# A decoder of two layers on one core: the order of VectorE's maxima in the up pass, and the place of three value-product copies

## The chip, the cores and the metric

The kernel runs on one core of a Trainium2 chip. The metric is device time in microseconds of one execution; lower is better. The median of three runs of the kernel before is 1388.31 us (1386.64 to 1389.0).

## The reference, cut to what matters

The whole program is a two-layer decoder on x of 8 x 512 x 256: linear attention, cross attention, a quantized feed-forward (FFN), then a metric attention, a second cross attention and a spectral FFN, each with a residual and a layer norm. The change lies in the feed-forward of layer 0:

```
act_qdq(x): scale = max(max|x| / 32767, 1e-12); clip(round(x / scale), ...) * scale   # one scale for the whole tensor
x    = act_qdq(x)
up   = act_qdq(x @ dequant(w_up).T)          # 8 batches of 512 x 768
gate = act_qdq(x @ dequant(w_gate).T)
sig  = round(sigmoid(gate) * 65536) / 65536, clipped
gate = act_qdq(gate * sig)                   # called t in the kernel before its scale is applied
o    = act_qdq(gate * up)
return o @ dequant(w_down).T
```

Every `act_qdq` needs the largest magnitude over all eight batches before one element can be rounded. That cuts the feed-forward into passes: gate, up, value (the product), down. The second cross attention needs, for each of 16 half head pairs, the product of context values with its output weights ("value products" 0 to 15); these depend on the context alone and are slipped into the passes of the feed-forward.

## The kernel before, in words

Each engine runs a queue of its own in the order in which its function issues work; the order is written out by hand, and engines meet at semaphores.

The **up pass** is the stage of the change. TensorE runs `up_pass(u, middle, after)` for u = 0 to 7: six up products of a batch (j = 0 to 5; each is four matmuls of 128x512 in the profile, L1092), with a small job after the third (middle) or after the sixth (after). Four PSUM banks take the up products in turn, so an up product waits for the copy of the one four before it. The small jobs are the projection of context values, `values(p)` (L1098), and `value_products(n)` (eight matmuls at L1118, two for each value pair), which write banks 6 and 7 and therefore wait until the copy of product n-1 has emptied them.

ScalarE copies the up products out (L1593: "early" is j = 0 to 2, "late" is j = 3 to 5), and between early and late of batch n it rounds the gate of batch n+1 (`gate_round`, L1598) and takes its sigmoid (`ffn_sigmoid`, L1603). Behind the late copies stand `copy_vw(n)` (L1633), which copies value product n to one buffer, and `copy_values(p)` (L1626). `copy_vw` also waits until the store of the product before it has left that buffer. A batch's first up copy waits for the up maximum two batches back, whose buffer it takes, and for its store; `gate_round(n)` waits for t of batch n-2.

VectorE does, for each batch: `gate_product` (L2249, L2250), which needs the batch's sigmoid and makes t in place; `t_peak` (L2255, L2256), the running maximum of t; `up_peak` (L2261, L2264), the running maximum of up, which needs all six up copies of the batch. The last batch's up maximum is taken in halves (`last_up_peak`, L2271). `peak(name)` (L2171) hands a maximum to GpSimd, which shares it over the partitions, and `scale` (L2179 to L2183) makes the scale from it.

SyncE's queue for this stage is: load the x of batch u+2, store up of batch u, store value product 8 + (u - 2), in turn (L621, L626, L561), each issue waiting for its input in this order.

Behind the up pass comes the **value stage**: ScalarE rounds up and t (L1701, L1693), VectorE multiplies them and takes the maximum (L2301, L2304), the last value products and the keys of the second cross attention are made beside it, and everything in it starts from the up scale. Then the down projection and layer 1 run in one loop over the batches. The value products 13 to 15 stand on ScalarE between the roundings.

Of the kernel before, what the change touches and what calls it, by code (L numbers as in the profile page):

```python
# [24 lines left out]
B, T, C = 8, 512, 256  # L25
# [146 lines left out]
def decoder(nc, x_in, pack_ident, pack_lin, pack_ctx, pack_xat, pack_ffn, pack_l1, pack_prep,  # L172
# [4 lines left out]
    with ctx:  # L177
# [46 lines left out]
        w.update(w1)  # L224
        layer1_end = ar.at
        l1_at = {n: sum(int(np.prod(d)) for _, d in PACK_L1[:i]) for i, (n, _) in enumerate(PACK_L1)}
        met_m = ar.take(NC, P)
        met_wo = ar.take(NC, C)
# [166 lines left out]
        def ev(name):  # L395

            if name not in sems:
                sems[name] = sem(name)
            return sems[name]
# [4 lines left out]
        def sig(name, per=1):  # L404

            if name not in sigs:
                if name in CONTINUES:
                    before = sig(CONTINUES[name], per)
                    sigs[name] = Signal(before.sem, per, before.base + B * per)
                else:  # L410
                    sigs[name] = Signal(sem(name), per)
            assert sigs[name].per == per, name
            return sigs[name]

        def wait(eng, name, b, j=None, per=1):

            s = sig(name, per)
            eng.wait_ge(s.sem, s.at(b, per if j is None else j))
# [28 lines left out]
        def vw_at(n):  # L447

            return 1 + n % 3 if n < VW_AHEAD else 0

        def vw_line(n):

            return ev(f"vw_stored_{max(1, vw_at(n))}")

        def vw_before(n):

            return sum(vw_line(m) is vw_line(n) for m in range(n))
# [5 lines left out]
        def wait_back(eng, name, b, back, per=1):  # L463

            if not b.before(back):
                eng.wait_ge(sig(name, per).sem, sig(name, per).at(b, per * (1 - back)))
# [30 lines left out]
        class Line:  # L497
# [5 lines left out]
            def link(self, ins):  # L503
                self.n += 1
                ins.then_inc(self.sem, 1)
                self.eng.wait_ge(self.sem, self.n)

        def rows2(k, n=2):

            return bank(k, n).rearrange("p a (b c) -> p (a b) c", c=C)  # L510
# [218 lines left out]
        def _(pe):  # L729
# [353 lines left out]
            def ffn_up_product(u, j):  # L1083
                n = NF * u + j
                if j == 0:
                    wait_moved(pe, "xt_loaded", Batch(u), u % 2, 2)
                if n < 4:
                    wait(pe, "gate_copied", Batch(B - 1), n + 1, NF)
                else:
                    wait(pe, "up_copied", Batch(0), n - 3, NF)  # L1090
                for k in range(NC):
                    last = mm(flat(2 + n % 4), wup_t[:, k, j * P:(j + 1) * P], ffn_xt[:, u % 2, k],  # L1092
                              start=k == 0, stop=k == NC - 1)
                last.then_inc(sig("up_done", NF).sem, 1)
# [51 lines left out]
            def up_pass(u, middle=None, after=None):  # L1146

                for j in range(NF):
                    ffn_up_product(u, j)
                    if j == NF // 2 - 1 and middle:  # L1150
                        middle[0](*middle[1:])
                if after:
                    after[0](*after[1:])
# [6 lines left out]
            up_pass(4, after=(values, 5))  # L1160
            up_pass(5, middle=(value_products, 10), after=(value_products, 11))
            up_pass(6, after=(values, 6))
            up_pass(7, middle=(value_products, 12), after=(value_products, 13))


            values(7)
# [279 lines left out]
        def _(act):  # L1446
# [140 lines left out]
            def ffn_copy_up(u, js):  # L1587
                if js[0] == 0:
                    wait_moved(act, "up_stored", Batch(u), u % 2, 2)
                    wait_back(act, "up_peaked", Batch(u), 2)  # L1590
                for j in js:
                    wait(act, "up_done", Batch(u), j + 1, NF)
                    f(ffn_up[:, u % 2, :, j], flat(2 + (NF * u + j) % 4).rearrange("p (t n) -> p t n", t=NT),  # L1593
                      ACT.Copy).then_inc(sig("up_copied", NF).sem, 1)

            def gate_round(n):
                wait_back(act, "t_ready", Batch(n), 2)
                f(gate_i[:, n % 2], gated[:, n], ACT.Copy, scale=quant["gate_mult"])\  # L1598
                    .then_inc(sig("gate_rounded").sem, 1)

            def ffn_sigmoid(n):
                wait(act, "gate_rounded", Batch(n))
                f(gated[:, n], gate_i[:, n % 2], ACT.Sigmoid, scale=quant["gate_scale"])\  # L1603
                    .then_inc(sig("sigmoid_done").sem, 1)
# [23 lines left out]
            def copy_vw(n):  # L1628

                act.wait_ge(ev("vw_done"), n + 1)  # L1630
                if vw_before(n):
                    act.wait_ge(vw_line(n), 32 * vw_before(n))
                f(vw_bufs[vw_at(n)].rearrange("p r i c -> p (r i) c"), rows2(6), ACT.Copy).then_inc(ev("vw_copied"), 1)  # L1633
# [27 lines left out]
            copy_values(4)  # L1661
            ffn_copy_up(3, early)
            gate_round(4)
            ffn_sigmoid(4)
            ffn_copy_up(3, late)
            copy_vw(8)
            ffn_copy_up(4, early)
            gate_round(5)
            ffn_sigmoid(5)
# [2 lines left out]
            copy_values(5)  # L1672
            ffn_copy_up(5, early)
            gate_round(6)
            ffn_sigmoid(6)
            ffn_copy_up(5, late)
            copy_vw(10)
            ffn_copy_up(6, early)
            gate_round(7)
            ffn_sigmoid(7)  # L1680
# [305 lines left out]
        def _(dve):  # L1986
# [183 lines left out]
            def peak(name):  # L2170
                v.tensor_copy(quant[name + "_max"], quant[name + "_max"]).then_inc(ev("peak_found"), 1)  # L2171
# [75 lines left out]
            def gate_product(n):  # L2247
                wait(dve, "sigmoid_done", Batch(n))
                link(v.tensor_scalar(sig_i, gated[:, n], 65536.0, 65535.0, ALU.mult, ALU.min))  # L2249
                v.tensor_tensor(gated[:, n], gate_i[:, n % 2], sig_i, ALU.mult).then_inc(sig("t_ready").sem, 1)  # L2250

            def t_peak(n):
                wait(dve, "t_ready", Batch(n))
                v.memset(spare, 0.0)
                link(v.tensor_reduce(quant["tmp"], gated[:, n], AX.X, ALU.max, apply_absolute_value=True))  # L2255
                link(v.tensor_tensor(quant["t_max"], quant["t_max"], quant["tmp"], ALU.max))  # L2256

            def up_peak(u):
                wait(dve, "up_copied", Batch(u), NF, NF)
                v.memset(spare, 0.0)  # L2260
                v.tensor_reduce(peaks[:, 0:1], ffn_up[:, u % 2].rearrange("p a b c -> p (a b c)"), AX.X, ALU.max,  # L2261
                                apply_absolute_value=True).then_inc(sig("up_peaked").sem, 1)
                wait(dve, "up_peaked", Batch(u))
                link(v.tensor_tensor(quant["up_max"], quant["up_max"], peaks[:, 0:1], ALU.max))  # L2264

            def last_up_peak():
                for n in range(2):
                    wait(dve, "up_copied", Batch(B - 1), NF * (n + 1) // 2, NF)
                    half = ffn_up[:, (B - 1) % 2].rearrange("p t j n -> p t (j n)")[:, :, n * FF // 2:(n + 1) * FF // 2]
                    v.memset(spare, 0.0)  # L2270
                    link(v.tensor_reduce(quant["tmp"], half, AX.XY, ALU.max, apply_absolute_value=True))  # L2271
                    last = v.tensor_tensor(quant["up_max"], quant["up_max"], quant["tmp"], ALU.max)
                    if n == 0:
                        link(last)
                last.then_inc(sig("up_peaked").sem, 1)
                wait(dve, "up_peaked", Batch(B - 1))

            first_gate_product()
            t_peak(0)
            up_peak(0)  # L2280
            for n in range(1, B - 1):
                gate_product(n)
                t_peak(n)
                up_peak(n)
            gate_product(B - 1)
            t_peak(B - 1)
            peak("t")
            last_up_peak()
            peak("up")
            scale("t", quant["t_raw"])  # L2290
# [383 lines left out]
```

## Time and profile before

| | |
|---|---|
| median of the runs | 1388.31 us |
| the profiled execution | 1386.88 us |
| its span, first to last instruction | 1385.1 us |
| mean granted TensorE clock | 0.957 |
| TensorE matmul busy | 1243.0 us (90%) |
| VectorE busy | 1046.8 us (76%) |
| ScalarE busy | 517.6 us (37%) |
| GpSimd busy | 267.7 us (19%) |

The span is the time from the first to the last instruction of one profiled execution, and all times of rows below are microseconds from its start. TensorE's busy share is that of matmuls, whose ends are modelled. The up pass lies between about 475 and 591 us, the value stage runs to about 663 us.

### The profile page before, as it was taken

What the parts mean: (1) busy time and instruction counts of PE and PEld (TensorE: products, weight loads), DVE (VectorE), ACT (ScalarE), POOL (GpSimd) and SP (SyncE); (2) the same over time, 40 slices, a digit from 0 to 9 for tenths busy, and PEclk for the clock granted to TensorE, in tenths of its full rate; (3) what the DMA queues carried; (4) which work ended last, traced back from release to release, by engine and by line L of the source; (5) the groups of instructions that cost most, each with busy time, mean ns of one, the idle gap of its engine ahead of it and who ended that gap; (6) DMA issues with size and microseconds to landing.
All of it is one profiled execution on the core that took longest, in us unless ns stands there. A gap on an engine that the chain in (4) does not pass through costs nothing.

```text
span 1385.1 us, 18416 instructions
## 1 busy us (share of the span) xinstructions
PE 1243.0 (90%) x7325; PEld 831.2 (60%) x7325; DVE 1046.8 (76%) x1949; ACT 517.6 (37%) x608; POOL 267.7 (19%) x189
## 2 busy tenths in 40 slices
PE   7899999997899999853679999999999999998976
PEld 4566666665544554321456686767767686766654
DVE  3578899987534779989554787978878797887767
ACT  1244343443534567588013332232323323241411
POOL 0011111112000000025100322314142141413242
PEclk9899999999999999976799999999999999999988
DMA  5000101102672044489322111111211000000000
GB/s 217 16 16 32 31 1 31 31 16 92 171 272 76 31 166 161 157 308 392 107 82 81 37 54 50 47 45 36 60 56 53 31 24 20 28 19 36 1 16 16
DMA packets 47829, 107.86 MB, mean 78 GB/s; under 512 B 10752, under 2 KB 31360, under 8 KB 44288
## 3 DMA queue, kind: packets, MB, share of 16 engines
q1 hardware_dynamic: 43584, 104.59, 21.7%
q10 hardware_dynamic: 4160, 2.10, 0.5%
q8 instruction: 59, 0.97, 0.3%
q14 instruction: 26, 0.21, 0.0%
HBM read 62.64 MB, written 44.04 MB: 77 GB/s over the span
## 4 chain that ended last, share of the span: by engine, by line
PE 74%; DVE 16%; ACT 4%; issue 2%; DMA 2%; POOL 0%; SPq 0%; POOLq 0%; ACTq 0%; DVEq 0%
PE ps L1313 8%; PE ps L1373 7%; PE ps L1199 6%; PE ps L1041 6%; PE ps L1092 4%; PE ps L795 4%; PE ps L1346 3%; PE ps L1258 3%; PE ps L943 2%; PE ps L1282 2%; PE ps L868 2%; PE ps L1293 2%; PE ps L1420 2%; PE ps L886 2%; PE ps L775 2%
## 5 line engine op out<-in xcount | busy, mean ns | idle before, releaser
L1373 PE MATMUL ps<-arena 128*128 128x256 f32 x512 | 120.3, 389 | 6.7 <-ACT arena L1836 6.7
L1313 PE MATMUL ps<-arena 128*128 128x512 f32 x256 | 117.6, 598 | 0.0
L1373 PEld LDWEIGHTS ps<-arena 128*128 128x128 f32 x512 | 98.5, 194 | 28.1 <-ACT arena L1836 10.0
L1874 POOL TENSOR_TENSOR arena<-arena 128x4 f32<-128x4 f32 x46 | 47.5, 1037 | 306.4 <-DVE arena L2049 306.4
L2389 DVE TENSOR_TENSOR arena<-ps,arena 128x2048 f32<-128x2048 f32 x32 | 73.3, 2291 | 39.1 <-PE ps L1258 38.9
L1935 POOL TENSOR_TENSOR arena<-arena 128x16 f32<-128x16 f32 x32 | 91.9, 2908 | 32.5 <-DVE arena L2418 32.5
L1199 PE MATMUL ps<-arena 128*128 128x256 f32 x384 | 89.4, 390 | 2.8 <-DVE arena L2342 2.8
L1041 PE MATMUL ps<-arena 128*128 128x512 f32 x192 | 85.5, 603 | 1.2 <-ACT arena L1564 1.2
L1092 PE MATMUL ps<-arena 128*128 128x512 f32 x192 | 84.7, 595 | 0.0
L1199 PEld LDWEIGHTS ps<-arena 128*128 128x128 f32 x384 | 73.9, 196 | 13.9 <-issue 3.9
L1313 PEld LDWEIGHTS ps<-arena 128*128 128x128 f32 x256 | 46.2, 190 | 48.7 <-issue 45.1
L1836 ACT ACTIVATE arena<-ps 128x1024 f32<-128x1024 f32 x32 | 32.8, 1026 | 111.9 <-PE ps L1360 111.9
L1346 PE MATMUL ps<-arena 128*128 128x128 f32 x512 | 65.8, 284 | 5.4 <-DVE arena L2432 5.4
L1815 ACT ACTIVATE arena<-ps 128x512 f32<-128x512 f32 x64 | 38.3, 599 | 85.0 <-PE ps L1313 85.0
L2055 DVE TENSOR_SCALAR arena<-arena 128x256 f32<-128x256 f32 x184 | 64.6, 418 | 4.7 <-POOL arena L1874 4.6
L1346 PEld LDWEIGHTS ps<-arena 128*128 128x128 f32 x512 | 62.7, 198 | 7.8 <-DVE arena L2432 7.1
L1881 POOL TENSOR_TENSOR arena<-arena 128x1024 f32<-128x1024 f32 x8 | 18.8, 2354 | 246.4 <-DVE arena L2109 246.4
L1041 PEld LDWEIGHTS ps<-arena 128*128 128x128 f32 x192 | 36.4, 193 | 44.6 <-issue 43.0
L1092 PEld LDWEIGHTS ps<-arena 128*128 128x128 f32 x192 | 36.1, 190 | 43.9 <-issue 41.6
L795 PE MATMUL ps<-arena 128*128 128x512 f32 x128 | 59.2, 597 | 1.3 <-ACT arena L1462 1.3
L2204 DVE TENSOR_REDUCE arena<-arena 128x1 f32<-128x3072 f32 (+1 forms) x9 | 26.9, 2994 | 35.6 <-issue 35.6
L2043 DVE BATCH_NORM_STATS2 arena<-arena 128x6 f32<-128x256 f32 x138 | 49.7, 416 | 4.5 <-POOL arena L1881 2.6
(281 smaller groups left out, 2628.1 us busy)
## 6 DMA issues: line engine op xcount, KB each, us to landing
v_scratch<-arena SPq DMA_DIRECT2D x7, 1536.0 KB, 13.5
arena<-v_scratch SPq DMA_DIRECT2D x7, 1536.0 KB, 6.8
up_scratch<-arena SPq DMA_DIRECT2D x6, 1536.0 KB, 6.6
arena<-up_scratch SPq DMA_DIRECT2D x6, 1536.0 KB, 10.9
vw_scratch<-arena SPq DMA_DIRECT2D x32, 256.0 KB, 3.9
arena<-x_scratch SPq DMA_DIRECT2D x16, 512.0 KB, 4.2
arena<-vw_scratch SPq DMA_DIRECT2D x8, 1024.0 KB
arena<-x SPq DMA_DIRECT2D x8, 512.0 KB, 5.7
```

Source lines behind the costliest of these rows:

```text
L795: last = mm(flat(t % 2), lin_xt[:, par, k, t * P:(t + 1) * P], w["lin_wkv"][:, k], start=k == 0, stop=k == NC - 1)
L1041: last = mm(flat(2 + j), wgate_t[:, k, j * P:(j + 1) * P], ffn_xt[:, par, k], start=k == 0, stop=k == NC - 1)
L1092: last = mm(flat(2 + n % 4), wup_t[:, k, j * P:(j + 1) * P], ffn_xt[:, u % 2, k], start=k == 0, stop=k == NC - 1)
L1199: last = mm(rows2(0 if b.early() else 5)[:, t], dn_v[:, t, j], wdown_t[:, j], start=j == 0, stop=j == NF - 1)
L1313: last = mm(flat(p % 2), w["cos_wq"][:, k, p * P:(p + 1) * P], xt4[:, k], start=k == 0, stop=k == NC - 1)
L1346: last = mm(flat(0, 2)[:, p * P:(p + 1) * P], cos_q[:, p, t * P:(t + 1) * P], cos_kb[:, par, p], start=True, stop=True)
L1373: last = mm(flat(2)[:, C:2 * C], cos_pt[:, p], cos_vw[:, par, p], start=p == 0, stop=p == NP - 1)
L1874: g.tensor_tensor(var[0], var[1], neghalf[:, 0:NT], ALU.pow)\
L1935: g.tensor_tensor(cos_nn[:, t, 0:H], cos_nn[:, t, 0:H], neghalf[:, 0:H], ALU.pow)\
L2043: v.bn_stats(st[:, t], r[:, t])
L2055: last = v.tensor_scalar(y[:, t], r[:, t], mv[:, t, 0:1], rs[:, t:t + 1], ALU.subtract, ALU.mult)
L2389: v.tensor_tensor(met_s[:, n % 2].rearrange("p r t h n -> p (r t h) n"), flat(3, 4).rearrange("p (h n) -> p h n", n=P), w["causal"].unsque ...
```

## The change

On TensorE value product 12 is taken from the middle of the last up pass and put behind it, with product 13 following. On ScalarE the copies of value products 8 and 10 move from behind the late up copies to between the gate's rounding and its sigmoid. On VectorE the up maximum of batch n-1 now follows gate product and t maximum of batch n, for n = 1 to 7; before, the up maximum of batch n followed those of batch n. The t peak is handed over ahead of the up maximum of batch 6. No instruction is added or taken away, and no wait is removed from a function.

```diff
@@ TensorE
             up_pass(6, after=(values, 6))
-            up_pass(7, middle=(value_products, 12), after=(value_products, 13))
+            up_pass(7, after=(value_products, 12))
+            value_products(13)
@@ ScalarE
             gate_round(4)
+            copy_vw(8)
             ffn_sigmoid(4)
             ffn_copy_up(3, late)
-            copy_vw(8)
             ffn_copy_up(4, early)
@@ ScalarE
             gate_round(6)
+            copy_vw(10)
             ffn_sigmoid(6)
             ffn_copy_up(5, late)
-            copy_vw(10)
             ffn_copy_up(6, early)
@@ VectorE
             first_gate_product()
             t_peak(0)
-            up_peak(0)
-            for n in range(1, B - 1):
+            for n in range(1, B):
                 gate_product(n)
                 t_peak(n)
-                up_peak(n)
-            gate_product(B - 1)
-            t_peak(B - 1)
-            peak("t")
+                if n == B - 1:
+                    peak("t")
+                up_peak(n - 1)
             last_up_peak()
             peak("up")
```

## Rows read from the trace of the kernel before

**Rows 1.** Stages: length, busy of PE, PEld, DVE, ACT, POOL; clock, DMA share, GB/s

```profile
487.10:590.60 103.50, 95.98 (x275) 46.59 (x273) 88.86 (x63) 67.15 (x70) 1.25 (x3) 1.00 0.49 167
590.60:662.70 72.10, 29.39 (x81) 15.08 (x81) 66.55 (x53) 55.88 (x30) 27.82 (x9) 0.68 0.89 335
```

**Rows 2.** Waits, 480 to 600 us: total us, times, longest us

```profile
PE ps L1118 <- ACT arena L1633: 13.3, 4, 6.8
DVE arena L2260 <- ACT arena L1593: 13.1, 5, 4.3
```

**Rows 3.** The chain of waits in the up pass: start us, us, what

```profile
531.53 0.92 ACT arena L1633
...
574.27 3.31 DVE arena L2261
```

**Rows 4.** ScalarE in order of time: start us, us, instruction, idle before it

```profile
501.45 2.85 ACT L1603 ACTIVATE arena<-arena 128x3072 f32<-128x3072 int16 x1
...
515.20 2.85 ACT L1603 ACTIVATE arena<-arena 128x3072 f32<-128x3072 int16 x1
...
524.34 2.85 ACT L1598 ACTIVATE arena<-arena 128x3072 int16<-128x3072 f32 x1
527.22 2.86 ACT L1603 ACTIVATE arena<-arena 128x3072 f32<-128x3072 int16 x1
529.98 1.55 ACT L1593 ACTIVATE arena<-ps 128x512 f32<-128x512 f32 x3
531.41 1.03 ACT L1633 ACTIVATE arena<-ps 128x1024 f32<-128x1024 f32 x1
...
542.48 2.85 ACT L1603 ACTIVATE arena<-arena 128x3072 f32<-128x3072 int16 x1
...
548.15 0.62 ACT L1593 ACTIVATE arena<-ps 128x512 f32<-128x512 f32 x1
...
554.50 2.86 ACT L1603 ACTIVATE arena<-arena 128x3072 f32<-128x3072 int16 x1
...
569.76 2.86 ACT L1603 ACTIVATE arena<-arena 128x3072 f32<-128x3072 int16 x1
...
584.82 0.60 ACT L1593 ACTIVATE arena<-ps 128x512 f32<-128x512 f32 x1 [1.12 <-PE ps L1092]
...
592.43 2.85 ACT L1701 ACTIVATE arena<-arena 128x3072 int16<-128x3072 f32 x1 [2.19 <-DVE arena L2183]
```

**Rows 5.** TensorE in order of time, the same columns

```profile
524.80 5.42 PE L1092 MATMUL ps<-arena 128*128 128x512 f32 x12
532.59 1.13 PE L1118 MATMUL ps<-arena 64*128 64x256 f32 x8 [2.37 <-ACT arena L1633]
...
596.34 2.08 PE L1118 MATMUL ps<-arena 64*128 64x256 f32 x8 [6.83 <-ACT arena L1633]
```

**Rows 6.** VectorE in order of time, the same columns

```profile
550.51 1.76 DVE L2249 TENSOR_SCALAR arena<-arena 128x3072 uint16<-128x3072 f32 x1
...
559.29 3.35 DVE L2261 TENSOR_REDUCE arena<-arena 128x1 f32<-128x3072 f32 x1
...
562.87 1.76 DVE L2249 TENSOR_SCALAR arena<-arena 128x3072 uint16<-128x3072 f32 x1
...
586.64 1.75 DVE L2271 TENSOR_REDUCE arena<-arena 128x1 f32<-128x1536 f32 x1
...
590.60 0.15 DVE L2171 COPY arena<-arena 128x1 f32<-128x1 f32 x1
```

**Rows 7.** SyncE's stores of value product 9; landing of these, then of all 32

```profile
547.74 1.18 SPq L561 DMA_DIRECT2D vw_scratch<-arena  x2
...
DMA to landing us min/median/max: 3.3/3.6/3.9
...
DMA to landing us min/median/max: 3.2/3.9/14.2
```

**Rows 8.** TensorE from 596 to 600 us: length, busy, granted clock, DMA share, GB/s

```profile
596.00:600.00 4.00, 3.66 (x10) 0.50 0.91 298
```

## The prediction, made before the changed kernel was run

> **What bounds the kernel now.** I read the busy time by stage first. The stretch from 487.10 to 590.60 us is the one the change edits: 103.5 us, in which TensorE is busy 95.98, VectorE 88.86 and ScalarE 67.15, at full TensorE clock [rows 1]. No engine is full, so the waits come next. Two groups stand out: TensorE's value products waited 13.3 us for the copy of the value product before them (6.83 of it lies after 590 us), and VectorE's up maximum waited 13.1 us, in five pieces, for the last up copies of its batch [rows 2]. The chain of waits shows how they join: it runs over TensorE and ScalarE, passes through the value-product copy at 531.53, and from 574.27 on it is VectorE without a gap [rows 3]. So TensorE and ScalarE set the pace in the middle, and VectorE's backlog sets the end. VectorE idles early for an up maximum whose input isn't there, while the next batch's sigmoid has been ready for some time, and pays this back at the end.
>
> The stage ends where the up peak is found, at 590.60; the scales and the whole value stage hang on it [rows 6].
>
> **Step 1: the copies of value products 8 and 10.** In batch 4's turn ScalarE rounds the gate at 524.34, takes the sigmoid at 527.22, the three late up copies at 529.98 and only then the value-product copy, at 531.41 [rows 4]. TensorE had finished its last up product of that pass at 524.80 + 5.42 = 530.22 and stood 2.37 us for that copy [rows 5]. Value product 8 itself was through by 524.80. After the change the copy starts behind the rounding, at about 527.1, and is done at about 528.1, 2.1 us before TensorE asks. The stall goes. The same pattern repeats one pair later (value product 11, also 2.37), so TensorE is 2.37 us earlier from batch 4's pass on and 4.74 from batch 6's. What is late next on TensorE is the bank rule (an up product needs the copy four products back): its late copies move to about 530.8 to 532.4, and the product that needs the first of them starts at 530.22 + 1.1 + 1.7 = 533.1. It doesn't wait.
>
> The price is paid by the sigmoid. Today it starts 527.22 - 524.34 = 2.88 after the rounding; with the copy between them it starts 2.76 (the pitch from 527.22 to 529.98) + 0.92 (the copy's step in the chain) = 3.68 after. So sigmoids 4 and 6 are 0.8 late against their own rounding. Sigmoid ends, from their starts + 2.85 [rows 4]: 530.08 becomes 530.9; batch 5's 545.33 becomes 542.96; 557.36 becomes 557.36 - 2.37 + 0.8 = 555.8; batch 7's 572.62 becomes 567.9.
>
> **Step 2: VectorE's order.** No instruction is added. The gate product and t maximum of one batch take 559.29 - 550.51 = 8.78 us, the up maximum 562.87 - 559.29 = 3.58, together 12.36 [rows 6]. With the new order the rows give this, a handover from the sigmoid taken at 0.03 (as between the rows at 524.34 and 527.22 of [rows 4]):
> batch 2 starts at sigmoid 501.45 + 2.85 + 0.03 = 504.33 and is through (with up maximum 1) at 516.69; batch 3 waits for its sigmoid, 515.20 + 2.88 = 518.08, until 530.44; batch 4 waits for its sigmoid, starts at 530.9, ends 543.3; batch 5 follows without a wait, to 555.6; batch 6 waits 0.2 for its sigmoid, 555.8, to 568.2; batch 7's product and t maximum end at 576.9, the t peak's copy adds 0.1, up maximum 6 ends at 580.6. The last up maximum in two halves takes 590.60 - 586.64 = 3.96, so the up peak is found at 584.6 instead of 590.6: **6.0 us earlier**.
>
> Each half alone, by the same bookkeeping: only the copies (old VectorE order) gives 586.1, a gain of 4.5, since VectorE still idles for up maximum 3 and again, briefly, for 5; only the order gives 589.0, a gain of 1.6, since sigmoid 7 then still ends at 572.6 and nothing can start before it.
>
> The moved up maximum also frees the up buffer two batches on, and ScalarE waits for that before the batch's first up copy. Up maximum 3 would end at 543.1, and the copy it frees stood at 548.15 [rows 4] and comes at 545.8: 2.7 us to spare, the smallest of these margins. The stores of up to memory read the buffer and wait for nothing of VectorE.
>
> **Step 3: value product 12 behind the last pass.** Its eight matmuls take 1.13 us, as product 9's [rows 5], ahead of the last three up products. Taken out of the middle, the last up copy ends at 585.42 (584.82 + 0.60, [rows 4]) - 4.74 - 1.13 = 579.6. The second half of the last up maximum wants it at 582.6. So this edit is worth nothing to the end, and TensorE and ScalarE have 3 us in hand there. Against it, products 12 and 13 now run one behind the other with a 1.03 us copy between: product 12 to 580.0, copy to 581.0, product 13 to 582.2, the value projection of four matmuls 1.8 more (a third of 5.42, [rows 5]), its copy about 0.7, done at about 584.7. The first rounding of up behind it in ScalarE's queue needs the up scale, 592.43 - 590.60 = 1.8 us after the up peak [rows 4, 6], at 586.4. It is covered by 1.7 us; each microsecond beyond that would come back in full.
>
> **The queues it passes.** SyncE keeps its order. Stores 8 and 10 are issued some 4 to 7 us sooner, and what stands behind them (the load for the next pass) still has TensorE's passes to wait for. ScalarE's new wait is copy 10 for the landing of store 9, one buffer: issued at 547.74 - 2.37 = 545.4, its second half 0.6 later, landing after 3.3 to 3.9 [rows 7], so at 549.9; it is asked for behind the rounding, 554.50 - 0.13 - 2.37 = 552.0 [rows 4]. Margin 2.1 us. Behind that wait stand sigmoid 6 and all of VectorE's last two batches.
>
> **The sum.** The stage ends 6.0 us earlier. Behind it nothing is edited, and all of it starts from the up scale: the value stage (72.1 us, [rows 1]) and the rest of the span should move as one block. Span 1385.1 - 6.0 = 1379.1, the profiled execution's 1386.88 becomes 1380.9, and the median of the runs, 1.4 above that execution, 1388.31 - 6.0 = **1382.3 us**.
>
> The Trainium skill, "Perfetto Trace Analysis", section Identifying the Most-Contended Engine, says to take the engine with the highest occupancy as the bottleneck and close its gaps (for TensorE it warns that matmul busy time flatters). In this stretch that is TensorE with 96 of 103.5 us [rows 1], and its two closed gaps sum to 4.74, where the chain gives 6.0. The rule bears on the first rival.
>
> **Rivals.**
> (a) TensorE's stalls are all there is to win: VectorE's new order brings nothing. Then the time is that of the copies alone, 4.5 us, 1383.8. For it: TensorE is the fullest engine. Against: the chain leaves TensorE at 574.27 [rows 3].
> (b) Only the order works, or the value stage gives back what is won, because the value copy stands in front of the first up rounding (step 3) or because memory traffic binds there (DMA share 0.89, [rows 1]): 1.6 us of gain, 1386.7. Against it: loads and stores of that stage are started by its own roundings and move with them.
> (c) TensorE's clock. Before value product 14 it idled 6.83 us and had fallen to the lower level, 1.2 GHz (0.50), which made that product 2.08 us instead of 1.13 [rows 5, 8], and the key products behind it slower too. I get an idle of about 6.3 us there, so no change. If the clock held, the 3.66 us of matmuls in the four microseconds at 0.50 [rows 8] would take half, 1.8 us more gain, 1380.5; as much again is my bound for what lies behind them, 1378.7.
> The Trainium skill, "TensorE: Matmul & The Clock Gate", Part 1, has the throttled state as the default, released by activity. By that rule the denser TensorE in the up pass can't be slower than today's 1.00, and the stretch behind it stays as it is.
> (d) Slower: store 9 lands late. ScalarE now asks for it ahead of sigmoid 6 and the late copies, not behind them. Each microsecond of landing beyond 6.0 holds sigmoid 6, VectorE's last two batches and the end one for one; beyond 12.0 the whole gain is gone. One such store took 14.2 [rows 7], which would be 8.2 - 6.0 = 2.2 us slower than before, 1390.5. Against it: that was in a stretch of heavier traffic, product 9's two landed in 3.3 and 3.9, and its neighbours in the queue stay the same ones.
> (e) The new order doesn't take hold, all within noise: 1388.3.
>
> **Chances.** The forecast 0.62 (its own range 1380.8 to 1383.2), (a) 0.16, (b) 0.09, (c) 0.06, (d) 0.03, (e) 0.04. A measurement here tells 0.2%, 2.8 us, from no change. (a), (c), the forecast and a quarter of (b), which may give back less than all, are faster: 0.87. The rest of (b) and (e) make 0.10 within it, (d) 0.03 slower. The range runs from inside the clock's case, 1379.5, to short of (b), at 1386.0.
>
> **What would show it.** Right: value products 9 and 11 follow the up products with no wait; VectorE's waits before the up maximum vanish and waits of some 4.3, 1.4 and 0.5 us appear before gate products 2, 3 and 4; no wait from there to the up peak but 0.2 before batch 6; the up peak at 584.6; sigmoid 4 3.7 us behind its rounding. Step 1 is wrong if either stall stays, step 2 if VectorE idles between batches 4 and 7, step 3 if the first up rounding starts more than 1.8 us behind the up peak. The forecast as a whole is wrong if the stage from the up peak to the first rounding of the down projection (72.1 us) grows by more than 1 us.

## The result, and the profile after

The changed kernel took 1378.16 us (median of four runs, 1377.12 to 1380.94) against 1388.07 us (four runs, 1386.64 to 1389.0); the ratio is 0.9933, with a 95% interval of 0.9914 to 0.9951. That is 9.9 us faster between the medians (9.3 between the means). The forecast was 1382.3 with a range from 1379.5 to 1386.0, so the time lies 1.3 us below the range, and the gain is larger than the 6.0 us forecast. Two of the later executions, the traced one of run e1 (1524 us) and one of run e8 (2180 us), ran at a mean granted clock of 0.83 and 0.55; they are left out of every number of this document.

The traced execution alone would have agreed with the forecast: span 1379.2 us (forecast 1379.1), its time 1380.94 us (forecast 1380.9), which is the slowest of the four. So the trace has to be read by stage, and it does not by itself explain the median. The stages after (length; busy time of PE, PEld, DVE, ACT and POOL; clock, DMA share, GB/s), the first from 487.10 to the end of the up scale, the second the value stage:

```profile
487.10:584.60 97.50, 93.83 (x267) 44.92 (x265) 89.27 (x73) 65.27 (x68) 3.66 (x4) 1.00 0.49 173
584.60:656.70 72.10, 29.97 (x80) 15.30 (x81) 64.94 (x44) 55.94 (x30) 27.94 (x8) 0.68 0.90 335
656.70:1379.20 722.50, 666.59 (x4449) 487.83 (x4449) 548.51 (x1197) 204.56 (x284) 185.07 (x137) 0.97 0.13 42
```

These windows start at fixed times, and the changed kernel reached the up pass earlier, so stages are better measured between events. I use three events on VectorE: the first t maximum, the up peak's copy, the value peak's copy. First the kernel before (the up peak's copy at 590.60 is in [rows 6]), then after (start us, us, instruction):

```profile
483.56 3.35 DVE L2255 TENSOR_REDUCE arena<-arena 128x1 f32<-128x3072 f32 x1
...
662.32 0.23 DVE L2321 COPY arena<-arena 128x128 f32<-128x128 f32 x1
```

```profile
481.74 3.35 DVE L2256 TENSOR_REDUCE arena<-arena 128x1 f32<-128x3072 f32 x1
...
582.72 0.15 DVE L2172 COPY arena<-arena 128x1 f32<-128x1 f32 x1
...
656.36 0.23 DVE L2320 COPY arena<-arena 128x128 f32<-128x128 f32 x1
```

The start is 1.8 us earlier (481.74 against 483.56), although nothing there was edited. The up pass went from 590.60 - 483.56 = 107.04 to 582.72 - 481.74 = 100.98 us, 6.06 less. The value stage went from 71.72 to 73.64, 1.9 more, and the rest from 722.78 to 722.84. In the value stage the difference is the load of up (chain of waits of the changed kernel):

```profile
602.25 13.72 DMA arena<-up_scratch
```

In the chain of the kernel before the same load is shorter:

```profile
610.34 11.59 DMA arena<-up_scratch
```

The start and the load cancel here by accident. What stands behind this load is alike in both traces: from its landing to the value peak's copy it is 662.32 - (610.34 + 11.59) = 40.39 us before and 656.36 - (602.25 + 13.72) = 40.39 after.

The waits of the changed kernel from 480 to 594 us, against [rows 2] (total us, times, longest us):

```profile
PE ps L1118 <- ACT arena L1634: 7.5, 2, 6.3
...
DVE arena L2250 <- ACT arena L1604: 7.0, 5, 4.3
```

TensorE's waits of 2.37 us are gone. VectorE no longer waits for up copies; it waits for sigmoids, 7.0 us instead of 13.1. ScalarE in order of time, against [rows 4]:

```profile
522.52 2.85 ACT L1599 ACTIVATE arena<-arena 128x3072 int16<-128x3072 f32 x1
525.26 1.01 ACT L1634 ACTIVATE arena<-ps 128x1024 f32<-128x1024 f32 x1
526.17 2.85 ACT L1604 ACTIVATE arena<-arena 128x3072 f32<-128x3072 int16 x1
528.91 1.57 ACT L1594 ACTIVATE arena<-ps 128x512 f32<-128x512 f32 x3
...
547.36 2.85 ACT L1599 ACTIVATE arena<-arena 128x3072 int16<-128x3072 f32 x1
550.10 1.01 ACT L1634 ACTIVATE arena<-ps 128x1024 f32<-128x1024 f32 x1
551.01 2.85 ACT L1604 ACTIVATE arena<-arena 128x3072 f32<-128x3072 int16 x1
...
584.55 2.85 ACT L1702 ACTIVATE arena<-arena 128x3072 int16<-128x3072 f32 x1 [1.69 <-DVE arena L2184]
```

The copy stands between rounding and sigmoid, and the sigmoid follows its rounding by 526.17 - 522.52 = 3.65 us (forecast 3.68). Copy 10, at 550.10, follows at the usual pitch: the landing of store 9 held nothing. TensorE, against [rows 5]:

```profile
522.98 5.42 PE L1092 MATMUL ps<-arena 128*128 128x512 f32 x12
528.33 1.13 PE L1118 MATMUL ps<-arena 64*128 64x256 f32 x8
529.39 10.57 PE L1092 MATMUL ps<-arena 128*128 128x512 f32 x24
...
579.10 1.13 PE L1118 MATMUL ps<-arena 64*128 64x256 f32 x8 [1.22 <-ACT arena L1634]
...
588.46 2.08 PE L1118 MATMUL ps<-arena 64*128 64x256 f32 x8 [6.32 <-ACT arena L1634]
```

Value product 9 (528.33) follows its pass without a wait. Product 14 again runs at half clock behind 6.32 us of idle.

VectorE, against [rows 6]; the waits before batches 2, 3, 4 and 6, the start of batch 5, and the end:

```profile
502.59 1.76 DVE L2250 TENSOR_SCALAR arena<-arena 128x3072 uint16<-128x3072 f32 x1 [4.33 <-ACT arena L1604]
...
516.34 1.76 DVE L2250 TENSOR_SCALAR arena<-arena 128x3072 uint16<-128x3072 f32 x1 [1.43 <-ACT arena L1604]
...
529.12 1.76 DVE L2250 TENSOR_SCALAR arena<-arena 128x3072 uint16<-128x3072 f32 x1 [0.46 <-ACT arena L1604]
...
541.48 1.76 DVE L2250 TENSOR_SCALAR arena<-arena 128x3072 uint16<-128x3072 f32 x1
...
553.97 1.76 DVE L2250 TENSOR_SCALAR arena<-arena 128x3072 uint16<-128x3072 f32 x1 [0.16 <-ACT arena L1604]
...
578.76 1.75 DVE L2272 TENSOR_REDUCE arena<-arena 128x1 f32<-128x1536 f32 x1
```

The last four of these times are the forecast's less 1.8 (530.9, 543.3, 555.8, 580.6).

### The profile page after: what moved, and what is told of

Its sections match the earlier page's. It is cut to its first block, busy times and chain, and to the rows that moved or that the text cites. A ratio compares the mean times of both kernels' runs of the same rounds, so it can differ in the third digit from the quotient of the medians.

```text
span 1379.2 us, 18416 instructions
## 1 busy us (share of the span) xinstructions
PE 1240.9 (90%) x7325; PEld 828.5 (60%) x7325; DVE 1046.5 (76%) x1949; ACT 517.5 (38%) x608; POOL 270.2 (20%) x189
## 4 chain that ended last, share of the span: by engine, by line
PE 74%; DVE 18%; ACT 3%; issue 3%; DMA 1%; POOL 1%; SPq 0%; ACTq 0%; POOLq 0%; DVEq 0%
PE ps L1314 8%; PE ps L1374 7%; PE ps L1200 6%; PE ps L1041 6%; PE ps L1092 4%; PE ps L795 3%; PE ps L1347 3%; PE ps L1259 3%; PE ps L943 2%; PE ps L868 2%; PE ps L1283 2%; PE ps L1294 2%; PE ps L1421 2%; PE ps L886 2%; PE ps L1189 2%
```

## Experiments

"The stretch" below is always the time from the first t maximum to the up peak. The theories as they stood when the experiments began: A, the up pass is 6 us shorter, by the steps of the prediction, and the rest is scatter; B, something outside the up pass is shorter too. C was added after the first four runs: each 2.37 us wait of TensorE also costs, in part of the executions, a fall of its clock behind the wait. The columns from the stretch on are from one trace of each kernel; "rest" is from the value peak's copy to the end.

| kernel | median us (runs) | ratio to before, 95% | stretch us | start to gate peak | value stage | rest |
|---|---|---|---|---|---|---|
| before, traced | 1388.07 (4) | | 107.04 | 473.7 | 71.7 | 722.8 |
| changed, traced | 1378.16 (4) | 0.9933 (0.9914 to 0.9951) | 100.98 | 471.8 | 73.6 | 722.8 |
| e1 changed again | 1379.52 (9) | 0.9952 (0.9934 to 0.9969) | | | | |
| e2 copies only | 1380.49 (6) | 0.9955 (0.9938 to 0.9972) | 102.47 | 473.9 | 72.3 | 719.7 |
| e3 order only | 1385.72 (12) | 0.9991 (0.9975 to 1.0006) | 108.75 | 471.9 | 72.6 | 723.0 |
| e4 product 12 in the middle | 1377.77 (7) | 0.9948 (0.9929 to 0.9967) | 100.98 | 469.4 | 71.4 | 723.2 |
| e5 order, filled | 1385.17 (12) | 0.9985 (0.9968 to 1.0002) | 105.55 | 471.9 | 72.8 | 723.9 |
| e6 before, filled | 1384.99 (12) | 0.9990 (0.9974 to 1.0007) | 107.05 | 471.6 | 71.8 | 723.4 |
| e7 order, widened | 1389.62 (10) | 1.0019 (1.0000 to 1.0037) | 111.04 | 473.6 | 70.8 | 723.0 |
| e8 before again | 1387.49 (9) | 0.9999 (0.9978 to 1.0020) | 108.76 | 472.1 | 73.8 | 723.0 |
| e9 value stage filled | 1377.23 (6) | 0.9930 (0.9915 to 0.9946) | 100.99 | 470.0 | 71.6 | 723.3 |
| e10 start filled | 1378.24 (6) | 0.9931 (0.9915 to 0.9947) | 100.99 | 469.6 | 71.6 | 723.1 |
| e11 both filled | 1379.10 (6) | 0.9939 (0.9922 to 0.9955) | 101.00 | 470.2 | 73.6 | 723.2 |
| e12 changed, third | 1378.76 (6) | 0.9936 (0.9920 to 0.9951) | 101.00 | 469.2 | 72.1 | 722.5 |
| f1 to f4 before | 1383.2, 1384.1, 1387.4, 1387.2 | | 107.05, 107.05, 110.35, 110.27 | 469.6 to 470.0 | 71.8 to 72.8 | 722.7 to 723.8 |

The shared runs of before were 1386.8 us in the first comparison (22 runs), 1386.7 in the second (35) and 1388.35 in the third (11). One more execution of before, untraced and beside f1 to f4, took 1379.2 us. So single executions of one kernel lie up to 16 us apart (1379.2 to 1395.6), and a difference of 2 us needs many of them.

### The parts of the change

e1 is the changed kernel unaltered.

> The changed kernel itself, unaltered, for a tighter time and a second trace. The trace of the changed kernel shows the up pass 6.1 us shorter (start of the first t maximum to the up peak: 107.0 before, 101.0 after), the value stage 1.9 us longer and the rest alike; yet the runs' median fell 9.9 us. Theory A (the up pass alone; the rest is scatter of the start and the value stage): with more runs the gain comes down to 5 to 8 us, and the second trace again has 101.0 us in that stretch. Theory B (something outside the up pass is also shorter in most runs, and the traced run missed it): the gain stays at 9 to 11 us.

Its median is 7.3 us below that of the 22 runs of before beside it (6.7 between the means), within A's 5 to 8. It has no trace to read, so the second trace of the changed kernel is that of e12.

e2, only ScalarE's edit:

```diff
             gate_round(4)
+            copy_vw(8)
             ffn_sigmoid(4)
             ffn_copy_up(3, late)
-            copy_vw(8)
...
             gate_round(6)
+            copy_vw(10)
             ffn_sigmoid(6)
             ffn_copy_up(5, late)
-            copy_vw(10)
```

> Only ScalarE's two moved copies; VectorE's order and product 12 as before. Theory A: TensorE's two waits of 2.37 us are gone and the up peak comes 4.5 us earlier counted from the first t maximum (102.5 us against 107.0); time 4.5 us below before, give or take 2. Rival (VectorE's backlog takes it all back): under 1 us. Theory B: 4 us more than A.

The stretch is 102.47 us, to 0.03 what A worked out. Its time is 6.3 us below before (6.0 between the means), where A had 4.5. By time alone it can't be told from the changed kernel (ratios 0.9955 and 0.9952); what the new order adds is seen in the stretch only, 102.47 - 100.98 = 1.49 us. The rest of its trace, 719.7 us, is 3 us shorter than in every other. Near the end four groups of 16 matmuls take 3.72 us each in e2; in each of the other traces of the table one takes about 6.1 or two take 5.41. So the clock near the end is another source of scatter, some 750 us behind the edit.

e3, only VectorE's edit (the loop as in the change, nothing on TensorE and ScalarE):

> Only VectorE's new order. Theory A: the two waits of 2.37 us stay, the up peak comes 1.6 us earlier (105.4 us from the first t maximum), time 1.6 us below before. Rival (a TensorE-bound stage, the order brings nothing): 0.0. Theory B, if the order is what moves the later stages: 5 us or more below before.

The stretch is 108.75 us, neither A's 105.4 nor the rival's 107.0. TensorE in order of time shows why:

```profile
530.81 1.13 PE L1118 MATMUL ps<-arena 64*128 64x256 f32 x8 [2.37 <-ACT arena L1633]
531.88 12.26 PE L1092 MATMUL ps<-arena 128*128 128x512 f32 x24
...
559.79 2.08 PE L1118 MATMUL ps<-arena 64*128 64x256 f32 x8 [2.37 <-ACT arena L1633]
561.79 11.12 PE L1092 MATMUL ps<-arena 128*128 128x512 f32 x24
```

24 up matmuls take 10.57 us in the changed kernel and 12.26 here, 1.7 more; behind the second wait value product 11 takes 2.08 instead of 1.13, and the matmuls 11.12. The same busy time by windows (length, TensorE busy, granted clock, DMA share, GB/s) has the lower level:

```profile
532.00:534.00 2.00, 2.00 (x3) 0.56 0.98 215
534.00:536.00 2.00, 2.00 (x4) 0.59 0.79 175
...
560.00:562.00 2.00, 2.00 (x9) 0.50 0.56 106
```

0.50 is 1.2 GHz, 1.00 is 2.4; 0.56 and 0.59 are means of windows that lie mostly at the lower level. In the one trace of before that the prediction had, the same two waits had left the clock at 1.00. This is theory C.

e4, the changed kernel with product 12 back in place:

```diff
-            up_pass(7, after=(value_products, 12))
-            value_products(13)
+            up_pass(7, middle=(value_products, 12), after=(value_products, 13))
```

> The changed kernel with value product 12 back in the middle of the last up pass. Theory A: the up peak is where the changed kernel has it (101.0 us from the first t maximum), last up copy about 1.1 us later; time equal to the changed kernel within 0.1%. Theory B: if product 12's place is what wins the extra 4 us (through the value products behind the pass), 3 to 4 us slower than the changed kernel.

The same stretch to 0.01 us. Its median is 1.8 us below that of e1, its ratio to before the same within either interval. So nothing here speaks for B, which had it 3 to 4 us slower, and product 12's place is worth nothing in the stretch.

### The wait and the clock

e5 and e6 put matmuls with no reader in front of value products 9 and 11, on the order alone and on the kernel before:

```diff
+            def fill(p):
+                for n in range(2):
+                    mm(flat(p % 2), ident, w["cos_wo"][:, 0:2], start=True, stop=True)
...
+                if u in (3, 5):
+                    fill(4 + (u == 5))
                 if after:
                     after[0](*after[1:])
```

> VectorE's new order alone, plus two full-size matmuls (four in the profile, 1.7 us) that write an unused bank in front of value products 9 and 11, so that TensorE stands 0.6 us instead of 2.37. In the trace of the order alone the clock fell to 0.50 behind each of these two waits and the stretch from the first t maximum to the up peak was 108.75 us, not the 105.4 expected. Theory C (the wait costs its 2.37 us and, in part of the executions, a fall of the TensorE clock behind it, which the copies' new place takes away): clock 1.00 from 500 to 590 us and 105.4 us for the stretch, time 1.6 to 3 us below before. Rival (the order itself costs the 3.3 us, through the up buffers that come free later): 108 to 109 us again, clock or no clock.

> The kernel before with the same filling matmuls. Nothing else is moved, and the filling ends before the copy that product 9 waits for, so it can't shorten the schedule at full clock. Theory C: 107.0 us for the stretch, clock 1.00, and a median 0 to 2 us below before, because the executions with a fallen clock go. Rival (no clock effect in the kernel before): median equal to before within 1 us, either sign.

TensorE in the order alone, filled:

```profile
528.27 1.88 PE L1148 MATMUL ps<-arena 128*128 128x512 f32 x4
530.80 1.13 PE L1118 MATMUL ps<-arena 64*128 64x256 f32 x8 [0.65 <-ACT arena L1639]
531.86 10.57 PE L1092 MATMUL ps<-arena 128*128 128x512 f32 x24
```

Value product 9 starts where it did in e3 (530.80 against 530.81), but the matmuls behind it take 10.57 us again. The stretch is 105.55, the 105.4 of the prediction's bookkeeping for the order alone, and 107.05 in the kernel before. So the order did not cost the 3.2 us (108.75 - 105.55); the clock did. The medians are blunter: e5 fell only 1.6 us below before, and e3 without the filling 1.1; the two can't be told apart. e6 is 1.7 us below before with an interval that includes none. That the falls are in the timed executions as they are in the traced ones is thus not shown by these two.

e7 makes copies 8 and 10 twice, on the order alone:

```diff
+                if n in (8, 10):
+                    f(vw_bufs[vw_at(n)].rearrange("p r i c -> p (r i) c"), rows2(6), ACT.Copy).then_inc(ev("mixer_copied"), 1)
+                    act.wait_ge(ev("mixer_copied"), n // 2 - 2)
                 f(vw_bufs[vw_at(n)].rearrange("p r i c -> p (r i) c"), rows2(6), ACT.Copy).then_inc(ev("vw_copied"), 1)
```

> The order alone with the copies of value products 8 and 10 made twice, so that each of the two waits on TensorE grows by 1.0 us, to 3.4. Theory C: the clock falls behind both in nearly every execution, and the stretch is 108 to 113 us, more than the 105.4 plus twice 1.0. Rival without a clock effect: 107.4 us or less.

```profile
533.62 1.24 PE L1118 MATMUL ps<-arena 64*128 64x256 f32 x8 [3.43 <-ACT arena L1636]
534.78 12.11 PE L1092 MATMUL ps<-arena 128*128 128x512 f32 x24
...
563.61 1.13 PE L1118 MATMUL ps<-arena 64*128 64x256 f32 x8 [3.43 <-ACT arena L1636]
564.67 12.26 PE L1092 MATMUL ps<-arena 128*128 128x512 f32 x24
```

Two of two waits of 3.43 us are followed by the slow level, and the stretch is 111.04, 5.5 more than in e5. Of that, 2.1 is the longer waiting and about 3.4 the two falls; e3, which also has both falls, is 2.3 shorter. One trace can't show that longer waits bring falls more often. The medians lean that way: e7 is 3.9 us slower than e3, and the longer waits explain 2.1 of it.

### How often it happens in the kernel before

> The kernel before, unaltered, as a kernel of its own: a second trace, and the size of the scatter. Theory A and C: its time is that of before within 0.2%. If the first trace of before was a lucky one (clock 1.00 through the up pass), this one shows 107 to 111 us from the first t maximum to the up peak; if there is no such scatter, 107.0 again. The other stages scatter too: the start up to the gate peak (469 to 474 us in five traces) and the value stage (71.4 to 73.6 us).

> The kernel before, one more trace of four. Of its two traces so far one shows a fall of the clock behind one of the two 2.37 us waits (108.76 us from the first t maximum to the up peak), one none (107.04). Theory C: over the four traces 3 to 5 of the 8 waits are followed by a clock of 0.50, each adding 1.0 to 1.7 us, so the mean of the stretch is 108 to 109 us. Rival (the two falls were rare, and the rest of the 7 to 8 us of gain is chance): at most 1 of 8.

> As for the first look: 107.0 without a fall, 108.0 to 108.8 with one, 109 to 110.5 with two.

f3 and f4 are the same kernel with the expectation of f2. TensorE in f3:

```profile
528.72 1.13 PE L1118 MATMUL ps<-arena 64*128 64x256 f32 x8 [2.37 <-ACT arena L1633]
529.78 12.26 PE L1092 MATMUL ps<-arena 128*128 128x512 f32 x24
...
557.70 2.08 PE L1118 MATMUL ps<-arena 64*128 64x256 f32 x8 [2.37 <-ACT arena L1633]
559.70 11.23 PE L1092 MATMUL ps<-arena 128*128 128x512 f32 x24
```

The six traces of the kernel before have 0, 1, 0, 0, 2 and 2 falls: 5 of 12 waits. The stretch is 107.04 or 107.05 without a fall, 108.76 with one, 110.27 and 110.35 with two, 108.42 on the mean; six traces fix that mean to a standard error of 0.7. f1 to f4 have 4 falls in 8 waits, as theory C expected, and not the rival's at most 1. The two waits of one execution are not independent: both or neither were followed by a fall in five of the six. The start up to the gate peak lies within 0.4 us in the four traces f1 to f4, and their times split as the falls do: 1383.2 and 1384.1 without, 1387.4 and 1387.2 with two. The changed kernel's two traces, e4, e9, e10 and e11 have no such wait, and a stretch of 100.98 to 101.00 us.

### The stages that were not edited

e9 fills the 6.3 us before value product 14, e10 two gaps near 35 and 41 us, e11 both, all on the changed kernel; e12 is the changed kernel beside them.

```diff
@@ e9, e11
             values(7)
+            for n in range(7):
+                mm(flat(0), ident, w["cos_wo"][:, 0:2], start=True, stop=True)
             value_products(14)
@@ e10, e11
+            def fill_start(n):
+                pe.wait_ge(ev("xat_v_biased"), 1)
+                for k in range(n):
+                    mm(flat(4), ident, w["lin_wkv"][:, 0], start=True, stop=True)
...
             def lin_state(b, par):
+                if b.first():
+                    fill_start(2)
...
+                    if t == 0 and b.first():
+                        fill_start(1)
                     if t == 0:
                         wait(pe, "lin_kv_ready", b)
```

> The changed kernel with seven filling products (fourteen matmuls of 128x512 in the profile, 6.0 us) into an unused bank, in the 6.3 us in which TensorE stands before value product 14. Theory: product 14 and the first key products then run at 1.00 instead of 0.50 (1.13 instead of 2.08, 7.0 instead of 8.6 us). If TensorE's clock sets the value stage, it is 1.8 to 3.6 us shorter, as bounded in the prediction's case (c). Rival: the stage is bound by memory traffic and by the roundings; it stays within its scatter of 70.8 to 73.8 us.

> The changed kernel with four filling matmuls ahead of the first batch's state product and two ahead of its first output product, in the two gaps of 1.92 and 0.86 us at 35 and 41 us. In the traces so far the clock there was 0.50 to 1.00 and the gate peak came at 469.4 (clock 1.00), 471.8 or 473.9 us. Theory C, applied to the start: the clock stays at 1.00 and the gate peak is at 469 to 470 in this trace; median 1 to 3 us below the changed kernel's. Rival (the start's scatter comes from the loads): 472 to 474 or spread as before.

> Both fillings on the changed kernel. If each does what its theory says, the time is the sum: 3 to 6 us below the changed kernel, about 1375. If only the start's does: 1 to 3 us below. If neither: equal.

> The changed kernel once more, as the base for the three beside it and as a second trace of it. Theory A with C: 101.0 us from the first t maximum to the up peak at clock 1.00, and a median 6 to 8 us below before; pooled with the runs so far 7.3.

e9 keeps the clock:

```profile
580.13 6.17 PE L1169 MATMUL ps<-arena 128*128 128x512 f32 x14
586.61 1.13 PE L1118 MATMUL ps<-arena 64*128 64x256 f32 x8 [0.31 <-ACT arena L1636]
587.68 7.13 PE L1135 MATMUL ps<-arena 128*128 128x512 f32 x16
```

against 2.08 and 8.75 us for the same rows in e12. The value stage is 71.6 us (e9) and 73.6 (e11), within its scatter. The chain of waits tells more. In all 17 traces of the table it passes the load of up, and from that load's landing to the value peak it is 40.38 to 40.50 us. So the whole scatter of the value stage is when this load lands, 30.4 to 33.4 us behind the up peak. With TensorE at full clock the load starts 17.5 (e9) and 17.7 us (e11) behind the up peak, against 19.4 to 19.5 in e10, e12 and the first trace of the changed kernel: the filling does move it forward by 1.8. But it then takes 13.70 and 15.33 us and lands at 31.2 and 33.1, no earlier than without (31.2, 31.7, 33.3). The prediction's case (c) put that gain at 1.8 to 3.6 us; two traces show none of it. e10 is inconclusive: the clock at the start was 1.00, and the gate peak at 469 to 470, in e12 and e9 too, without the filling. In the timed runs the fillings beat the changed kernel by nothing that six runs each can tell; e11, with both, is the slowest of the four.

## Why the prediction was wrong

**Step 1, the copies: right, with one term left out.** Both waits went and the sigmoid's 3.65 us came as worked out; in e2 the stretch is 102.47 against 102.5 forecast. The step that failed is the worth of a wait. The prediction priced each at its 2.37 us, because in its one trace the stage ran "at full TensorE clock", and its sentence on the clock gate held that the denser TensorE "can't be slower than today's 1.00", taking that 1.00 for the kernel's state. It was one execution's. Over six traces the two waits cost another 108.42 - 107.04 = 1.4 us on the mean (standard error 0.7), in the clock behind them; on the traces' terms the gain is then 108.42 - 100.99 = 7.4 us, not 6.0. For e2 the same sum gives 108.42 - 102.47 = 6.0 us, which is what its means show, where the forecast had 4.5. Case (c), the clock, was looked for only behind the pass, where giving it back won nothing.

**Step 2, VectorE's order: right.** The stretch fell by 6.06 us where neither trace has a fall (forecast 6.0); the waits before batches 2, 3, 4 and 6 are 4.33, 1.43, 0.46 and 0.16 (forecast 4.3, 1.4, 0.5 and 0.2). Each half alone gave, at full clock, 4.6 (e2, forecast 4.5) and 1.5 (e5, forecast 1.6). Rival (a), that the order brings nothing, falls in the stretch, where e2 and the changed kernel differ by 1.49 us; the times don't tell the two apart.

**Step 3, product 12: right.** Worth 0.00 (e4), and the first up rounding stood 1.83 us behind the up peak (584.55 - 582.72).

**The queues and rival (d): right that it doesn't happen.** Nothing waited for store 9.

**"Behind it nothing is edited and should move as one block": right on average, but not in one execution.** The prediction's own sign against it, a value stage longer by more than 1 us, did appear in the first pair of traces (71.72 and 73.64). It was the scatter: six traces of before have 72.3 on the mean, four of the change (the first, e4, e10, e12) 72.2. The start scatters from 469.2 to 473.9 us and the value stage from 70.8 to 73.8, though nothing is edited there but in e9, e10 and e11. For the start its steps come with the clock: the state product at 37 us takes 2.05 us in the nine traces with a gate peak at 469.2 to 470.2, 3.4 to 3.5 in the five at 471.6 to 472.1, and 3.81 in the three at 473.6 to 473.9. For the value stage it is the landing of the load of up, in all 17 traces; why that load takes 11.1 to 15.3 us wasn't tried.

**The median.** The changed kernel was timed beside before three times, and the means lie 9.3, 6.7 and 9.1 us apart. Weighted by their spread they give 8.4 us, give or take 1.2. The traces' 7.4 agrees with that; the 6.0 of the prediction doesn't. The first comparison's 9.9 us is these 7.4 and about 2.5 more from four runs a side; the interval of its ratio reaches from 6.8 to 11.9 us. That this last part is chance is an inference, and its cause stays open: the start, the landing of the load and the clock near the end move single executions by 2 to 5 us, and no trace shows which of them, or how many falls, the other timed runs had. The forecast also took its median of before (1388.31, three runs) 1.5 us above the mean of the 68 later runs (1386.8). With the missing term in it the forecast would have been 1388.31 - 7.4 = 1380.9, inside its range, and still 2.7 us above the measured median.

## What to carry to other kernels

A wait of the matrix engine costs its length and, in some executions, a stretch at half clock behind it; one trace shows only one of the outcomes, so where a change closes or opens such a wait, look at several traces or price both. Where two engines take turns being late, moving the consumer's next ready work ahead of what isn't ready and freeing the producer have to be summed through one schedule: apart they gave 4.6 and 1.5 us, together 6.06. The schedule written out from the rows hit each to 0.1, at full clock. Where a stage not edited gets longer or shorter, find the one event it hangs on before calling it an effect: here each value stage was the landing of one load plus 40.4 us. A median of four runs on a kernel whose runs spread by 7 us and more can be 2 us off (an estimate from that spread).

## What the runs showed of the hardware

- Of fourteen TensorE waits of 2.37 us between dense stretches (six traces of before, one of the order alone), seven were followed by the 1.2 GHz level, seven weren't; of two waits of 3.43 us both; of four of 0.65 us none. In twelve traces with a wait of 1.69 us, before value product 13, the matmuls behind it ran at full speed; but only 3 us of them follow before the next wait, so that a later fall wouldn't be seen. Near 37 us the state product, behind a wait of 1.92 us (and one of 0.89 shortly before), ran partly or wholly slow in 8 of 15 traces without a filling there. So the length of the wait alone doesn't decide it.
- One fall costs 1.6 to 1.7 us of the stretch here: 24 matmuls of 128x512 took 12.26 us instead of 10.57.
- The Trainium skill, "TensorE: Matmul & The Clock Gate", Part 1, has throttling as the default that activity releases. The rows agree: the granted clock is 1.00 where TensorE is busy 93.83 of 97.50 us, and 0.68 where it is busy 29.97 of 72.10. The same part calls the warm-up variable from run to run, since what watches the activity runs free of the program. Here the fall varies too: f1 to f4, one kernel on one chip with the start equal to 0.4 us, gave no fall, no fall, two and two.
- Matmuls with no reader, placed in a wait, left the clock at 1.00 for what follows (e5, e6, e9, e11) and delayed nothing, since they ended before the wait did. Before value product 14 this is clear: it took 2.08 us in all 15 traces without the filling, behind 5.3 to 7.1 us of idle, and 1.13 in both with it. For the waits of 2.37 us it rests on two traces, and the kernel unfilled also ran without a fall in three of six.
- The load of up that the value stage's chain of waits passes took 11.1 to 15.3 us in 17 traces, while the time from its landing to the value peak was always 40.4 to 40.5 us.
